# Two more tiles of each batch in three rounded terms, and the next batch's first seed read straight from PSUM

## The reference

```python
def attention(x, context, mask, Wq, Wkv, Wout, bout):
    k, v = jnp.split(context @ Wkv, 2, axis=-1)
    q = x @ Wq
    q, k, v = (_split_heads(q), _split_heads(k), _split_heads(v))
    dots = jnp.einsum('bhnd,bhmd->bhnm', q, k) * SCALE
    dots = dots - (1.0 - mask.astype(jnp.float32))[:, None, :, None] * MASK_NEG
    attn = jax.nn.softmax(dots, axis=-1)
    out = jnp.einsum('bhnm,bhmd->bhnd', attn, v)
    b, h, n, d = out.shape
    return out.transpose(0, 2, 1, 3).reshape(b, n, h * d) @ Wout + bout

def ffn(x, w1, b1, w2, b2):              # 8 experts, one per batch
    tokens = x.reshape(E, T, D)
    h = jax.nn.gelu(jnp.einsum('etd,edf->etf', tokens, w1) + b1[:, None, :])
    return (jnp.einsum('etf,efd->etd', h, w2) + b2[:, None, :]).reshape(B, S, D)

x = x + attention(_layernorm(x), ctx_1024, mask_BxS_ik0, Wq, Wkv, Wout, bout)
x = x + ffn(_layernorm(x), w1, b1, w2, b2)
```

## Time and profile before

| | |
|---|---|
| median of 3 runs | 375.22 us (374.8 to 375.67) |
| the profiled execution | 374.87 us, its span 373.0 us |
| PE busy | 363.0 us, 97% |
| DVE, ACT, POOL busy | 75%, 68%, 31% |
| granted clock of PE, mean | 0.995 of full speed |
| chain of work that ended last | PE 85%, DVE 10%, no wait shown 2%, ACT 1% |

### The profile page before, as it was taken

One profiled execution on the slowest core, in us unless ns is written; L12 is line 12 of the kernel. 1 busy time (PEld: TensorE's weight loads), 2 busy tenths in 40 slices (PEclk: granted clock), 3 DMA queues, 4 the chain that ended last, 5 costly groups with the idle time before them and its releaser, 6 DMA issues.

```text
span 373.0 us, 5778 instructions
## 1 busy us (share of the span) xinstructions
PE 363.0 (97%) x1713; PEld 278.7 (75%) x1713; DVE 279.3 (75%) x458; ACT 255.1 (68%) x335; POOL 116.1 (31%) x125
## 2 busy tenths in 40 slices
PE   6899999999999999999999999999999999999996
PEld 6767777777777887777777877777777877687755
DVE  4888677978797669878797669878797669454863
ACT  3556576697769576697679476697579467796621
POOL 1610573245324430145324440255224440022000
PEclk9999999999999999999999999999999999999998
DMA  7686268329932854339932764349933752438400
GB/s 239 216 195 176 54 129 199 85 83 168 201 94 82 150 98 134 82 104 235 233 88 86 144 113 117 84 117 235 222 86 100 129 108 40 119 68 156 74 2 6
DMA packets 30622, 47.10 MB, mean 126 GB/s; under 512 B 2011, under 2 KB 21371, under 8 KB 30608
## 3 DMA queue, kind: packets, MB, share of 16 engines
q0 software_dynamic: 9936, 27.40, 37.6%
q1 hardware_dynamic: 20672, 19.52, 17.5%
HBM read 24.59 MB, written 0.23 MB: 67 GB/s over the span
## 4 chain that ended last, share of the span: by engine, by line
PE 85%; DVE 10%; issue 2%; ACT 1%; DMA 1%; SPq 0%; DVEq 0%; ACTq 0%
PE ps_s L444 29%; PE ps_a L484 23%; PE ps_x L500 10%; PE ps_a L477 9%; PE ps_x L533 3%; PE ps_a L421 2%; PE ps_x L553 2%; PE ps_x L458 1%; DVE shift_diag L930 1%; DVE ex_sum L900 1%; DMA ex_all<-in_wk_t 1%; PE ps_x L562 1%; DVE chunk_max L919 1%; DVE ex_lo L915 1%; PE ps_x L530 1%
## 5 line engine op out<-in xcount | busy, mean ns | idle before, releaser
L919 DVE TENSOR_REDUCE chunk_max<-ps_x 128x1 f32<-128x500 f32 x168 | 111.1, 677 | 31.9 <-PE ps_x L500 28.8
L708 ACT ACTIVATE ex_all<-ps_s 125x896 f32<-125x896 f32 x95 | 87.1, 917 | 44.1 <-PE ps_s L444 42.7
L484 PE MATMUL ps_a<-ex_all,ctx_sb 125*128 125x448 f32 x248 | 110.9, 541 | 0.0
L726 ACT COPY ps_s<-shift_row 125x896 f32<-125x896 f32 x94 | 85.7, 911 | 12.2 <-DVE shift_row L1057 9.7
L500 PE MATMUL ps_x<-ctxt_hi,qk_hi 128*128 128x500 f32 x168 | 80.7, 484 | 1.1 <-DVE chunk_max L919 0.9
L1234 POOL DMA_DIRECT2D ex_all<-ex_all x48 | 42.2, 878 | 115.9 <-ACT ex_all L708 111.6
L444 PE MATMUL ps_s<-qk_hi,ctxt_hi 128*125 128x448 f32 x192 | 76.3, 479 | 0.0
L484 PEld LDWEIGHTS ps_a<-ex_all,ctx_sb 125*128 125x128 f32 x248 | 46.3, 190 | 17.1 <-issue 12.7
L444 PE MATMUL ps_s<-qk_hi,ctxt_lo 128*125 128x448 f32 x192 | 54.9, 367 | 0.0
L444 PE MATMUL ps_s<-qk_lo,ctxt_hi 128*125 128x448 f32 x192 | 54.7, 366 | 0.0
L444 PEld LDWEIGHTS ps_s<-qk_hi,ctxt_hi 128*125 128x125 f32 x192 | 35.9, 187 | 24.4 <-issue 23.3
(11 more groups left out here) (110 smaller groups left out, 382.1 us busy)
## 6 DMA issues: line engine op xcount, KB each, us to landing
ex_all<-ex_all POOLq DMA_DIRECT2D x48, 448.0 KB, 4.6
ctxt_raw<-in_ctx_t SPq DMA_DIRECT2D x8, 750.0 KB, 6.5
ctx_sb<-in_ctx SPq DMA_DIRECT2D x8, 750.0 KB
ctxt_hi<-in_ctx_t POOLq DMA_DIRECT2D x21, 250.0 KB, 3.1
w_sb<-in_w SPq DMA_DIRECT2D x4, 512.0 KB, 5.0
w_sb<-in_w SPq DMA_DIRECT2D x8, 256.0 KB, 6.6
ex_all<-in_wq_t SPq DMA_DIRECT2D x2, 256.0 KB, 3.8
ex_all<-in_wk_t SPq DMA_DIRECT2D x2, 256.0 KB, 4.8
```

The source lines that it names most:

```text
L484: mm = nc.tensor.matmul(ps_a[:, c, 0:CH], ctx_sb[0:MT, u, t, :], ex(t)[0:MT, c * CH:(c + 1) * CH], start=(slot == 0), stop=(slot == TM - 1))
L708: nc.scalar.activation(half(ex(t)[0:MT, :]), src, ACT.Exp, scale=SCALE).then_inc(ex_ready, 1)
L726: nc.scalar.copy(ps_s[0:MT, t % 2, :, 0:CH], half(shift_row[0:MT, b.parity, :])).then_inc(seeded, 1)
L919: nc.vector.tensor_reduce(chunk_max[:, k, t:t + 1], filled()[:, 0:MC], AX.X, ALU.max).then_inc(job_free, 1)
```

## The change

Three things. First, tiles 0 and 10 join `SPLIT`, so all even tiles go in three rounded terms (in the last batch, tile 10 stays float32); the last two slots change places, and tile 0 now opens the accumulation. `ctx_hi` and `ctx_lo` grow from four tiles to six. For the first batch, `ctx_hi` is now made ahead of the drains of the later queries. Second, ACT seeds the first tile of every batch but the first from the banks of `ps_x` that the shift's matmuls fill, and then copies `shift_row` itself, in place of DVE; `sum_hi` takes the room of `shift_diag`, and is made one step later. Third, the maximum at (2, 2) goes, and one at (9, 1) comes.

```diff
-    SPLIT = [2, 4, 6, 8]
-    PV_ORDER = [0, 1, 2, 3, 5, 4, 7, 6, 9, 8, 10, 11]
+    SPLIT = [0, 2, 4, 6, 8, 10]
+    PV_ORDER = [0, 1, 2, 3, 5, 4, 7, 6, 9, 8, 11, 10]
...
-        [(1, 0), (1, 1), (1, 2), (2, 0), (2, 1), (2, 2), (4, 0), (4, 1), (4, 2), (5, 0), (5, 1), (5, 2),
-         (6, 0), (6, 1), (6, 2), (7, 0), (7, 1), (7, 2), (8, 0), (8, 2), (9, 0)],
+        [(1, 0), (1, 1), (1, 2), (2, 0), (2, 1), (4, 0), (4, 1), (4, 2), (5, 0), (5, 1), (5, 2),
+         (6, 0), (6, 1), (6, 2), (7, 0), (7, 1), (7, 2), (8, 0), (8, 2), (9, 0), (9, 1)],
...
-    ADD_AT = {(10, 2): (0,), (11, 0): (1, 2)}
-    ADD_LATE = (3, 4)
+    ADD_AT = {(10, 2): (0,), (11, 1): (1, 2)}
+    ADD_LATE = {(0, 0): (3, 4)}
+    LOW_AT = [(t + 1, 1) for t in SPLIT[:-1]] + [(11, 0)]
...
-        sum_hi = sb("sum_hi", [P, Q], F32R)
+        sum_hi = shift_diag[:, :, :].rearrange("p t q -> p (t q)")
...
+        def buffer_free(n):
+
+            return read_by(SPLIT[n - 2]) if n >= 2 else read_by(SPLIT[SPLITS - 2 + n]) - TM
...
                             mm = nc.tensor.matmul(ps_a[:, c, 0:CH], a[0:MT, u, n, :], e[0:MT, n % 2, c * CH:(c + 1) * CH],
-                                                  start=False, stop=False)
+                                                  start=(slot == 0 and term == 0), stop=(slot == TM - 1 and term == 2))
...
+            def first_seed(b):
+
+                act.wait_ge(job_ready, jobs.value())
+                act.wait_ge(ex_ready, b.at(TM, -1))
+                nc.scalar.copy(ps_s[0:MT, 0, :, 0:CH], ps_x[0:MT, :, 0:CH]).then_inc(seeded, 1)
+                nc.scalar.copy(half(shift_row[:, b.parity, :]), ps_x[:, :, 0:CH]).then_inc(job_free, 2)
...
                     if t == 1 and b.off > 0:
+                        sum_high_part(b.later(-1))
                         att_out(b.later(-1))
+                    if prepare and t == TM - 2:
+                        ex_high_part(b, SPLITS - 1)
...
                             jobs.n = FIRST_JOBS if first else jobs.n + 2
+                            first_seed(b.later(1))
...
-                    if t == 0 and b.off > 0:
-                        sum_high_part(b.later(-1))
-                    if t == 1 and first:
-                        ctx_high_part(b)
...
             drain_queries(3)
+            ctx_high_part(Batch(None, 0))
             for h in range(HEADS):
                 drain_later_queries(h)
...
                     if prepare and at == SHIFT_AT:
-                        shift_copies(b.later(1))
+                        jobs.n += 2
...
-                    if b.i is None and b.off == 0 and t == 2:
+                    if b.i is None and b.off == 0 and t == 0:
                         ctx_low_part(b)
```

More of the change, by code:

```diff
@@ L566, in shift_jobs @@
             def shift_jobs():
-                for c in range(2):
+                for _ in range(2):
+                    c = jobs.n % 2
                     shift_rows(job()[:, 0:CH], P, c, start=True).then_inc(job_ready, 1)
@@ L713, in ex_high_part @@
                 act.wait_ge(ex_ready, b.at(TM, t + 1))
-                if n >= 2:
-                    act.wait_ge(pv_done, b.at(TM, read_by(SPLIT[n - 2])))
+                wait(act, pv_done, b.at(TM, buffer_free(n)))
                 nc.scalar.copy(ex_hi[0:MT, n % 2, :], ex(t)[0:MT, :]).then_inc(ex_hi_ready, 1)
@@ L807, in iteration @@
                             jobs.n = FIRST_JOBS if first else jobs.n + 2
+                            first_seed(b.later(1))
+                        else:
                             act.wait_ge(job_free, jobs.value())
-                        seed(b.later(1), t + 2 - TM)
-                    if t == 0 and b.off > 0:
-                        sum_high_part(b.later(-1))
-                    if t == 1 and first:
-                        ctx_high_part(b)
+                            seed(b.later(1), 1)
                     if t == CTX_HI_AT and prepare:
                         ctx_high_part(b.later(1))
-                    if t in SPLIT:
+                    if t in SPLIT[:-1]:
                         ex_high_part(b, SPLIT.index(t))
@@ L913, in ex_low_part @@
                 dve.wait_ge(ex_hi_ready, b.at(SPLITS, n + 1))
-                wait(dve, pv_done, b.at(TM, read_by(SPLIT[n - 2]) if n >= 2 else read_by(SPLIT[n - 2]) - TM))
+                wait(dve, pv_done, b.at(TM, buffer_free(n)))
                 nc.vector.tensor_tensor(ex_lo[0:MT, n % 2, :], ex(SPLIT[n])[0:MT, :], ex_hi[0:MT, n % 2, :].bitcast(F32),
@@ L1053, in shift_copies @@
             def shift_copies(b):
-                wait(dve, seeded, b.at(TM, -TM - 2))
-                for c in range(2):
+                for _ in range(2):
+                    c = jobs.n % 2
                     nc.vector.tensor_copy(shift_row[:, b.parity, c * CH:(c + 1) * CH], filled()[:, 0:CH]).then_inc(job_free, 1)
@@ L1109, in add @@
                 def add(at):
-                    if at == (0, 0) and b.off > 0:
-                        for n in ADD_LATE:
-                            add_to_sum(b.later(-1), n)
+                    for n in ADD_LATE.get(at, ()) if b.off > 0 else ():
+                        add_to_sum(b.later(-1), n)
                     for n in (ADD_AT if prepare else LAST_ADD_AT).get(at, ()):
                         add_to_sum(b, n)
-                    if (at[0] - 1, at[1]) in [(t, 1) for t in SPLIT]:
-                        ex_low_part(b, SPLIT.index(at[0] - 1))
+                    if at in LOW_AT and (prepare or LOW_AT.index(at) < SPLITS - 1):
+                        ex_low_part(b, LOW_AT.index(at))
                 for t in range(TM):
@@ L1260, in iteration @@
                     if prepare and t == 6:
-                        pool.wait_ge(ex_lo_ready, b.at(SPLITS, 2))
+                        pool.wait_ge(ex_lo_ready, b.at(SPLITS, 3))
                         ctxt_lo_chunk(b.later(1), 1)
@@ L1265, in iteration @@
                     if prepare and t == 8:
-                        pool.wait_ge(ex_lo_ready, b.at(SPLITS, 3))
+                        pool.wait_ge(ex_lo_ready, b.at(SPLITS, 4))
                         ctxt_lo_chunk(b.later(1), 2)
```

## The result

The changed kernel takes 384.58 us (median of 4 runs, 383.78 to 386.24), the kernel before 375.01 us beside it: a ratio of 1.026, with an interval of 1.022 to 1.030. It is slower, and by more than I forecast (380.2, range 377.0 to 382.8).

The account below looks back on a forecast made before the run. PE, busy 97% of the span, was taken as the bound: 374.87 - 4.05 (three terms) + 3.85 (context wait) + 1.5 (clock) + 1.0 (first batch) + 3.0 (moved maximum) = 380.2 us, range 377.0 to 382.8.

Parts of the forecast that it names:

- the four waits: PE's added losses: context wait 3.85 us, low clock 1.5, first batch's low part 1.0, moved maximum 3.0.
- What the three terms save: Tile 0 in eight batches and tile 10 in seven save PE 0.27 us each, 4.05 us taken whole.
- What that costs elsewhere, hidden: Fifteen added high parts on ACT (14 us) and low parts on DVE (16 us) stay far under PE's 363.
- What the early `ctx_hi` costs: Prologue: ACT casts batch 0's context before the later drains, so PE stands 3.85 us, bounds 2.6 to 4.2.
- the lag behind the last packet: Prologue: the context load lands later than its last packet, by at most 1.1 us, judged from the load of `w_out`.
- What the stop does to the clock: After the prologue stop PE's granted clock falls to 0.50, costing 1.5 us; nothing to 2.7 possible.
- What the first batch's low part costs: Batch 0: tile 0's low part stands between two maxima on DVE, so PE stands 1.0 us before job (2, 1).
- What the moved maximum costs: Batch boundaries: the maximum at (9, 1) lengthens PE's wait before the shift by 0.43 us, seven times, 3.0 us.
- The rivals: Four alternatives: context in time (0.04), boundary free (0.11), PE time alone counts (0.04), ACT late (0.11).
- the context came in time: Prologue rival: `ctx_sb` lands by 17.0, so context wait and clock fall vanish; 374.8 us, chance 0.04.
- ACT was not late with `att`: Rival at batch start: `att` comes 0.4 us late for PE's slot 0 in seven batches; 383.0 us, chance 0.11.
- The first seed: Batch start: ACT's seed comes sooner behind the shift's matmuls, covered by 3.2 us of PE work; cost nothing.

Follow-up runs that it names:

- E11: Changed kernel with the three mends of E8, but tiles 0 and 10 back in float32 (four tiles in three terms): 373.34 us.
- E8: Changed kernel with E5's and E6's edits, and batch 0's context cast in two halves ahead of drains 8 and 10: 371.55 us, ratio 0.991.
- E6: Changed kernel, POOL's first chunk of the next batch's context low part held until DVE made the low part of tile 2 (batches 1 to 6): 383.18 us.
- E9: E8 with the maxima in their places of before, (2, 2) back and (9, 1) gone: 372.41 us, ratio 0.993.
- E1: Changed kernel with the cast of batch 0's context on ACT moved behind fourteen of the sixteen drains of the later queries: 379.69 us.
- E3: Changed kernel with DVE's low part of tile 0 moved from (1, 1) to (1, 2), behind the third maximum and `sum_lo`: 388.75 us.
- E2: Kernel before with only the cast of batch 0's context moved ahead of the sixteen drains: 381.43 us.
- E7: Changed kernel with 14 idle matmuls on PE ahead of the third later query, where PE waits for the context: 384.42 us.
- E10: Changed kernel with 20 idle matmuls on PE ahead of the third later query, where PE waits for the context: 382.99 us.
- E4: Changed kernel with the maxima in their places of before, (2, 2) back and (9, 1) gone: 382.15 us.
- E5: Changed kernel with DVE's low part of tile 8 moved behind the shift, to (10, 0), except in the last batch: 379.3 us.
- E12: Kernel before with only DVE's low part of tile 8 moved behind the shift, to (10, 0): 372.92 us, ratio 0.994.

## Why the prediction was wrong

The direction and the four waits were right. The size was not: 4.4 us too low, outside the range.

- **What the three terms save**: right. 0.54 us forecast in a batch, 0.53 in E11 against E8.
- **"What that costs elsewhere, hidden"**: this step failed. I priced 15 low parts at 1.09 us on an engine with room, and asked only whether DVE has the time. What the low part of tile 0 pushes back is `sum_lo`, and with it POOL, whose subtraction then holds up the low part of tile 2 on DVE: 0.85 us, six times. PE waited 0.74 more in each pair batch and 0.13 in the plain ones, 2.6 us by the trace. The collision makes 1.9 of these (E6; 1.4 in the medians). The other 0.23 of each pair batch, 0.7 in all, is saved time that does not last: PE comes to step 4 sooner by more than DVE does, and waits there (3.81 without the collision, 3.58 in E9 and E11, where PE comes later). I had counted what waits behind the new instruction on DVE in the first batch alone, and took PE's saving whole. The Trainium skill has the rule, page "SBUF — State Buffer", section "Who interferes with whom": a DVE instruction with two inputs in SBUF contends with a GpSimd instruction that reads SBUF, and the order of issue decides which of them is blocked. The traces agree in both directions: DVE waits for POOL (1.94 for 1.09, E1's 1.36 for 0.17), POOL for DVE (E3's 2.93 for 2.27).
- **What the early `ctx_hi` costs**: right in kind, too small. I put the landing at 20.7 us and bounded it at 21.1; the cast began at 22.27 here, and in the six experiments that kept the early cast in the changed kernel between 20.8 and 23.3 from one execution to the next. That single trace of before could not bound a landing which varies by 2.5 us. The term that failed is the lag behind the last packet, bounded at 1.1 us by the load of `w_out`. The changed kernel's packets to 20.3 us:

```profile
DMA packets 3321, 4.77 MB, mean 235 GB/s; under 512 B 454, under 2 KB 2082, under 8 KB 3321
```

2082 - 454 = 1628, so all of the prediction's packets were through by then, and the cast began 2.0 us later; in the six experiments it began 1.1 to 2.8 us behind the last of them. PE's third query matmul ran at 23.49 rather than 22.1, 5.24 us later than before where 3.85 were forecast.
- **What the stop does to the clock**: right in kind. 1.5 us were forecast; the execution profiled lost 2.7, those of E2 to E7 between 1.35 and 2.5, and keeping PE busy saved 1.6 in the median (E10). The whole prologue, 5.35 forecast, cost 7.9 in the profile and 6.3 to 6.65 in medians (E8, E2).
- **What the first batch's low part costs**: right. Batch 0 took 1.17 us more; the terms of the sum made 1.16 (1.0 + 0.43 - 0.27).
- **What the moved maximum costs**: right. Step 10 grew by 0.53 and 0.36 in the two batches shown, where 0.43 was forecast, and by 3.3 us over the seven boundaries for 3.0. That E4 gave 2.4 does not show this price: by its trace only 1.2 comes from the places of the maxima, since (2, 2) has a price of its own now, and the rest from steps 4 and 5. E5, which takes DVE's work off the boundary, shows that DVE's run sets the wait.
- **The rivals**: the context came in time in no execution profiled. ACT was not late with `att`: step 2 takes 2.9 us, which is its work, the scores, two maxima and a split tile (1.23 + 0.44 + 1.23). The first seed, costed at nothing, cost nothing that shows: steps 11 and 0 of the loop are as long as before.

The miss of 4.4 us is then some 3.0 in the loop (2.6 in steps 4 and 5, 0.3 in step 10), about 1.0 in the prologue, and the rest small terms that I did not separate.

## What to carry to other kernels

Before work is put on an engine that "has room", follow what it pushes back, engine by engine, to the next pair of instructions that must not meet; a margin of 0.01 us in the trace of before is a warning. Ask also where the engine that is made faster will wait next: 0.23 us a pair batch went back in step 4. A wait for a load belongs behind all work that others need from the same engine, and its cost is bounded by more than one execution. Where DVE releases PE at a handover, look first for work ahead of the release that is wanted only later: that one move (E12, 2.0 us) was worth as much as the two tiles (E11, 1.8).

## What the hardware showed that I had not expected

DVE and POOL shut each other out nearly to the end of an instruction: seven columns on DVE took 1.36 us instead of 0.17, ending with POOL's subtraction of 768 columns. The granted clock stayed at 0.50 for some 6 us after PE was fully busy again, from 23.5 to 29.5, and for 3.3 to 5.6 us in those of E2 to E7; behind stops of 2.51 us (E7) and 3.35 it fell, behind one of 1.44 (E10) it did not. In E5, behind a stop of 3.78 us, it fell 1.1 us after PE had resumed.
